# The passage from sampling to attention in a four-image hybrid block: image 0's last two tiles projected alone, the other images' projections behind the second scores

## The reference, cut to what matters

```python
x = x + _L0_conv_ref(_gn(x), ...)        # ends: out @ out_w + out_b
t = _to_tokens(x)                        # (4, 1024, 128)
t = t + _L1_attn_ref(_ln_t(t), W)        # x = n @ W; softmax(x @ n.T / sqrt(128)) @ n
t = t + _L1_ffn_ref(_ln_t(t), ...)       # router, two experts, gelu, layer norm
```

## Time and profile before

| | us |
|---|---|
| median of 3 runs | 721.9 (720.75 to 722.38) |
| profiled execution, its own time | 724.42 |
| its span, first to last instruction | 722.7 |
| mean granted clock of PE in it | 0.908 of full |

### The profile page before, as it was taken

One profiled execution on the slowest core, in us unless ns is written; L12 is line 12 of the kernel. 1 busy time (PEld: TensorE's weight loads), 2 busy tenths in 40 slices (PEclk: granted clock), 3 DMA queues, 4 the chain that ended last, 5 costly groups with the idle time before them and its releaser, 6 DMA issues.

```text
span 722.7 us, 11093 instructions
## 1 busy us (share of the span) xinstructions
PE 593.9 (82%) x3456; PEld 444.2 (61%) x3456; DVE 580.6 (80%) x1052; ACT 227.1 (31%) x332; POOL 306.8 (42%) x326
## 2 busy tenths in 40 slices
PE   4982878869859869869959589779999999939995
PEld 3452656557547558557547477647777777725674
DVE  4489899998997997998999999456777766752766
ACT  6150502413314314215206000144445444413431
POOL 7523795897348793058068240021221221125111
PEclk9796988998998987988999779989999999977998
DMA  6057503003003006000000000000000000004111
GB/s 182 29 212 269 169 1 103 3 1 103 1 1 103 2 2 254 1 1 2 1 1 3 0 1 1 1 0 1 1 1 1 1 0 1 1 3 115 30 45 44
DMA packets 25595, 30.54 MB, mean 42 GB/s; under 512 B 5189, under 2 KB 17685, under 8 KB 25557
## 3 DMA queue, kind: packets, MB, share of 16 engines
q1 hardware_dynamic: 24654, 29.77, 12.5%
q0 software_dynamic: 896, 0.23, 0.4%
q10 hardware_dynamic: 6, 0.00, 0.0%
HBM read 24.94 MB, written 5.05 MB: 42 GB/s over the span
## 4 chain that ended last, share of the span: by engine, by line
PE 55%; DVE 20%; issue 10%; DVEq 2%; ACT 1%; POOL 0%; POOLq 0%; ACTq 0%
PE banks L777 14%; DVE prod L1355 9%; PE banks L887 8%; PE pair L867 8%; PE pair L932 4%; PE pair L730 4%; PE banks L877 4%; PE banks L966 3%; DVE stencil L1331 3%; DVE outer L1325 3%; PE banks L795 3%; PE pair L723 2%; PE banks L793 2%; PE banks L859 1%; DVE hats L1292 1%
## 5 line engine op out<-in xcount | busy, mean ns | idle before, releaser
L777 PE MATMUL banks<-ident,prod 128*128 128x128 f32 x1568 | 225.2, 295 | 81.5 <-DVE prod L1355 80.8
L777 PEld LDWEIGHTS banks<-ident,prod 128*128 128x128 f32 x1568 | 192.7, 152 | 136.1 <-DVE prod L1355 112.5
L1355 DVE TENSOR_TENSOR prod<-shifted,stencil 128x1024 f32 (+1 forms) x224 | 238.8, 1089 | 17.3 <-PE banks L777 14.5
L1123 POOL CAST far_list_i<-far_list 1x8 int32<-1x8 f32 x8 | 40.5, 5066 | 105.5 <-DVE far_list L1341 86.1
L1151 POOL TENSOR_TENSOR rstd_now<-mv_now,neg_half 128x2 f32<-128x2 f32 x32 | 22.9, 717 | 135.6 <-DVE mv_now L1407 135.6
L730 PE MATMUL pair<-xg,dw_diag 128*128 128x512 f32 x144 | 73.4, 611 | 1.7 <-ACT dw_diag L511 1.7
L887 PEld LDWEIGHTS banks<-shifted 128*128 128x128 f32 x512 | 60.2, 192 | 8.1 <-issue 6.1
L887 PE MATMUL banks<-shifted 128*128 128x128 f32 x512 | 63.3, 277 | 2.3 <-ACT shifted L639 1.4
L1325 DVE TENSOR_TENSOR outer<-hats 128x800 f32<-128x800 f32 x64 | 63.2, 987 | 0.8
L1331 DVE TENSOR_TENSOR stencil<-stencil,outer 128x800 f32 (+1 forms) x64 | 62.9, 983 | 0.3
L867 PE MATMUL pair<-shifted 128*128 128x512 f32 x128 | 60.4, 596 | 0.6 <-ACT shifted L622 0.6
(11 more groups left out here) (229 smaller groups left out, 871.6 us busy)
## 6 DMA issues: line engine op xcount, KB each, us to landing
shifted<-padded SPq DMA_DIRECT2D x42, 256.0 KB
shifted<-padded SPq DMA_DIRECT2D x14, 640.0 KB
res<-in_x_dram SPq DMA_DIRECT2D x4, 512.0 KB, 5.7
padded<-stage SPq DMA_DIRECT2D x4, 512.0 KB, 2.7
stage<-in_L_ffn_W_dram SPq DMA_DIRECT2D x16, 128.0 KB, 2.1
out_dram<-res SPq DMA_DIRECT2D x8, 256.0 KB, 2.3
padded<-stencil SPq DMA_DIRECT2D x2, 228.0 KB, 2.5
got<-padded,cell_now POOLq DMA_INDIRECT x28
```

What stands on the lines that cost most here:

```text
L777: mm = pe.matmul(acc_of(c, r), prod[:, d % PROD, r * G:(r + 1) * G, :].rearrange("p g c -> p (g c)"), ident[:, :], is_transpose=True, star ...
L1123: gp.tensor_copy(far_list_i[:, :], far_list[:, :]).then_inc(point, 1)
L1355: ins = ve.tensor_tensor(prod[:, dx:dx + n, :, :], shifted[:, dx:dx + n, bass.ds(((c % HALF) * ROWS + dy) * G, ROWS * G), :], stencil_of[: ...
```

## The change

The projection of the last two chunks (6 and 7) is split by image. Behind `add_fix` of chunk 7, PE projects image 0 of chunk 6 and then image 0 of chunk 7, three matmul calls each; chunk 7 has its own copy of samples (`samp_last`, behind `samp_t` in `xg`) and its own bank (bank 1), so ACT makes both sample copies one behind the other. Two residual copies of one tile follow (`res1_first`). DVE waits for the residuals of chunks 0 to 5 ahead of the first statistics, for `res1_first` ahead of those of pair 3, and for all residuals ahead of the attention loop. On PE the transposes and keys of image 0 come first, then the scores of tile 0, the keys of pair 3, the scores of tile 1, the projections of images 1 to 3 of both chunks, and then pairs 4 and 5. ACT has the residuals of images 1 to 3 between the two exponentials. The banks of pairs 2 and 3 move from `pair[0]` to `pair[1]`.

```diff
-            first = [bank[2], bank[3], pair[0][:, 0:512], pair[0][:, 512:1024], bank[2], bank[3]]
+            first = [bank[2], bank[3], pair[1][:, 0:512], pair[1][:, 512:1024], bank[2], bank[3]]
...
-            for k in (CHUNKS - 2, CHUNKS - 1):
-                copy_out(k)
-                residual(k)
+            def residual_of(k, n0, n1):
+                at = k % 2
+                sc.activation(res[:, :, :].rearrange("p (n k) c -> p n k c", n=B)[:, n0:n1, k, :],
+                              bank[at][:, n0 * P:n1 * P].rearrange("p (n c) -> p n c", c=C), ACT.Copy
+                              ).then_inc(res1_first if n0 == 0 else res1_done, 1)
+
+            copy_out(CHUNKS - 2)
+            copy_out(CHUNKS - 1)
+            for i, k in enumerate((CHUNKS - 2, CHUNKS - 1)):
+                sc.wait_ge(conv_first, i + 1)
+                residual_of(k, 0, 1)
...
             copy_normed(0)
-            for j in range(LEAD):
-                if j + 1 < LEAD:
-                    copy_normed(j + 1)
+            copy_normed(1)
+            copy_keys(0)
+            copy_normed(2)
+            copy_keys(1)
+            copy_normed(3)
+            copy_keys(2)
+            copy_keys(3)
+            exps(0, 0)
+            for i, k in enumerate((CHUNKS - 2, CHUNKS - 1)):
+                sc.wait_ge(conv_out, CHUNKS - 1 + i)
+                residual_of(k, 1, B)
+            exps(1, 1)
+            for j in (4, 5):
+                copy_normed(j)
                 copy_keys(j)
-                if j == 3:
-                    exps(0, 0)
-                    exps(1, 1)
...
-            def project(k):
+            def project(k, n0=0, n1=B):
+                last = isinstance(k, int) and k == CHUNKS - 1
                 pe.wait_ge(samp_t_done, k + 1)
-                pe.wait_ge(res1_done, k + 1)
-                for n in range(B):
-                    y = bank[0][:, n * P:(n + 1) * P]
+                pe.wait_ge(res1_done, CHUNKS - 1 if last else k + 1)
+                if n0 > 0:
+                    pe.wait_ge(res1_first, 2 if last else 1)
+                for n in range(n0, n1):
+                    y = bank[1 if last else 0][:, n * P:(n + 1) * P]
...
-            add_up(CHUNKS - 1, AT_SAMPLES, AT_PROJECT)
-            project(CHUNKS - 2)
-            add_up(CHUNKS - 1, AT_PROJECT, STENCIL)
+            add_up(CHUNKS - 1, AT_SAMPLES, STENCIL)
             add_fix(CHUNKS - 1)
-            project(CHUNKS - 1)
+            project(CHUNKS - 2, 0, 1)
+            project(CHUNKS - 1, 0, 1)
...
             normed_to_t(0)
-            for j in range(LEAD):
-                if j + 1 < LEAD:
-                    normed_to_t(j + 1)
+            pe.wait_ge(samp_t_done, CHUNKS)
+            normed_to_t(1)
+            keys(0)
+            normed_to_t(2)
+            keys(1)
+            normed_to_t(3)
+            keys(2)
+            pe.wait_ge(normed_t1, TILES // 2)
+            pe.wait_ge(keyed_done, 1)
+            scores(0, 0)
+            keys(3)
+            pe.wait_ge(keyed_done, TILES // 2)
+            scores(1, 1)
+            project(CHUNKS - 2, 1, B)
+            project(CHUNKS - 1, 1, B)
+            for j in (4, 5):
+                normed_to_t(j)
                 keys(j)
-                if j == 3:
-                    pe.wait_ge(keyed_done, 4)
-                    scores(0, 0)
-                    scores(1, 1)
+            pe.wait_ge(res1_done, CHUNKS + 1)
...
-            ve.wait_ge(res1_done, CHUNKS + 1)
+            ve.wait_ge(res1_done, CHUNKS - 1)
...
+                    if j + 1 == TILES // 2 - 1:
+                        ve.wait_ge(res1_first, 2)
                     token_stats(j + 1, 2 * ((j + 1) % 2), var1)
...
             maxima(1, 1)
+            ve.wait_ge(res1_done, CHUNKS + 1)
```

More of the change, by code:

```diff
@@ L240, in hybrid_block_kernel @@
         fix = over_stage[:, :].rearrange("p (s g c) -> p s g c", s=CHUNKS, c=CG)
-        samp_t = xg[:, :, :, :].rearrange("p y w n -> p (y w n)")[:, 0:CT].rearrange("c (n r w) -> c n r w", n=B, r=ROWS)
+        samp_t, samp_last = [xg[:, :, :, :].rearrange("p y w n -> p (y w n)")[:, s * CT:(s + 1) * CT]
+                             .rearrange("c (n r w) -> c n r w", n=B, r=ROWS) for s in range(2)]
         over_shifted = shifted[:, :, :, :].rearrange("p d s c -> p (d s c)")
@@ L350, in hybrid_block_kernel @@
         res1_done = sem("res1_done")
+        res1_first = sem("res1_first")
+        conv_first = sem("conv_first")
         var1 = sem("var1")
@@ L560, in copy_out @@
                 sc.wait_ge(samp_tp, k + 2)
-                sc.activation(samp_t, banks[:, bass.ds(512 + (k % 2) * 1024, 512)].rearrange("c (r w n) -> c n r w", r=ROWS, n=B),
+                sc.activation(samp_last if isinstance(k, int) and k == CHUNKS - 1 else samp_t, banks[:, bass.ds(512 + (k % 2) * 1024, 512)].rearrange("c (r w n) -> c n r w", r=ROWS, n=B),
                               ACT.Copy).then_inc(samp_t_done, 1)
@@ L786, in add_fix @@
                 mm.then_inc(samp_tp, 1)
-            def project(k):
+            def project(k, n0=0, n1=B):
+                last = isinstance(k, int) and k == CHUNKS - 1
                 pe.wait_ge(samp_t_done, k + 1)
-                pe.wait_ge(res1_done, k + 1)
-                for n in range(B):
-                    y = bank[0][:, n * P:(n + 1) * P]
-                    pe.matmul(y, samp_t[:, n, :, :].rearrange("c r w -> c (r w)"), out_w_sb[:, :], start=True, stop=False)
+                pe.wait_ge(res1_done, CHUNKS - 1 if last else k + 1)
[3 more added lines that the diff above has]
+                    y = bank[1 if last else 0][:, n * P:(n + 1) * P]
+                    pe.matmul(y, (samp_last if last else samp_t)[:, n, :, :].rearrange("c r w -> c (r w)"), out_w_sb[:, :],
+                              start=True, stop=False)
                     pe.matmul(y, ones16[0:3, :], bias_parts3[:, 3 * GP:], start=False, stop=False)
                     mm = pe.matmul(y, ident[:, :], res[:, n * TILES + k, :], start=False, stop=True)
-                mm.then_inc(conv_out, 1)
+                mm.then_inc(conv_out if n1 == B else conv_first, 1)
             pe.wait_ge(gate_done, 1)
```

## The result

| | before | after |
|---|---|---|
| median of 7 runs, us | 721.9 (719.71 to 724.77) | 717.2 (716.22 to 721.9) |
| ratio, 95% interval | | 0.995 (0.9927 to 0.9973) |
| profiled execution, us | 724.42 | 716.8 |
| its span, us | 722.7 | 714.9 |
| mean granted clock of PE | 0.908 | 0.921 |

The forecast was 717.7. A ratio of 0.995 is 3.6 us, between 1.9 and 5.3. The two profiled executions differ by 7.6 us (their spans by 7.8), and that is not the change's doing alone: the last product ended at 458.99 us before and at 454.42 after, in code that no edit touches. Of the 7.8 us the passage up to the loop's first scores gave 3.00, the sampling stage ahead of it 4.57, the rest 0.23.

A forecast was written before the change was run, and what follows sets the result against it. Latency of the chain from sampling's last product to the attention loop was taken as the bound: 10.85 us gained at the first scores less 6.65 given back is 4.2, so 721.9 - 4.2 = 717.7 us, range 716.0 to 720.9.

The forecast's parts named there:

- Reading the chain: From the last sampling product to the attention loop's first turn: latency bounds; bringing the loop forward brings the end forward equally.
- Step 1, DVE's start: DVE's first statistics, waiting only for chunks 0 to 5, begin at 459.05 instead of 467.98: 8.93 us earlier.
- Step 2, PE and ACT ahead of the norm: Behind the last products: sample copy from 460.36, one-tile residuals by 462.32, transpose of pair 0 at 461.81, costing nothing.
- Step 3, the first scores: First scores behind the norm of pair 3 start at 467.26 against 478.11: 10.85 us earlier, full clock kept.
- Step 4, what is given back: Between first scores and loop, 6.65 us given back, most of it 4.80 of projections; keys of pair 5 at 480.41.
- The hole of 0.6 ahead of the second scores: PE waits about 0.6 us, as the copy of pair 3's keys now follows the first scores.
- ACT's in-order price: Tile 1's exponential, free to run at 473.3, stands behind both residuals on ACT until 477.44 and ends at 478.54.
- The sum: Keys of pair 5 at 480.4 instead of 484.64: 4.2 us less, bounds 3.8 to 4.5.
- the first rival: Half clock before the scores or at 477.1 to 480.4: costs 1.75 us, gain 2.45, time 719.4; chance 0.25.
- the second thin place: Stretch 477.1 to 480.4 ahead of the loop, where PE has only two pairs' short work; half clock possible there.
- the first sparse stretch: Norm passage before the scores, PE working 0.82 us of each 1.50 for four pairs; full clock assumed.
- the prediction's own list: Signs to check: first scores 10.9 us earlier, probability transposes about 4.2 earlier; wrong if half clock from the first scores on.

The follow-up runs named there:

- the two experiments on single orders: Changed kernel with pair 3's keys ahead of the first scores, 716.77 us; changed kernel with tile 1's exponential ahead of both residuals on ACT, 718.40 us.
- both experiments that kept the two gaps: Changed kernel with DVE's first statistics waiting for both one-tile residuals, 726.01 us; changed kernel with pair 3's keys ahead of the first scores, 716.77 us.
- keys of pair 3 first: Changed kernel with the keys of pair 3 ahead of the first scores on PE, all else as changed; 716.77 us in its one run.
- the split alone: Changed kernel with DVE waiting for both one-tile residuals ahead of its first statistics, all else as changed; 726.01 us in its one time.
- exponential first: Changed kernel with the exponential of tile 1 ahead of the two residuals on ACT instead of behind them; 718.40 us in its one run.
- The second set of runs: Kernel before, changed kernel and kernel before with only DVE's waits changed, 12 runs each on one chip: medians 722.06, 719.11 and 718.46 us.
- early start: Kernel before with only DVE's waits changed: chunks 0 to 5 ahead of first statistics, all residuals ahead of pair 3's; 716.27 us, ratio 0.9941.

## Why the prediction was right, step by step

*Reading the chain.* That the passage is a chain of latencies, and that what it loses comes off the end, held: from the loop's scores to the end 236.42 after, 236.65 before, a difference smaller than the 1.8 us by which this stretch varies over the twelve profiles.

*Step 1, DVE's start.* Forecast 8.93 us earlier; 9.07 by distance (8.99 against -0.08). The row of the statistics begins 0.08 before that of the last product ends.

*Step 2, PE and ACT ahead of the norm.* Forecast: transpose of pair 0 at 2.82 behind the last product; measured 3.01. The one-tile residuals took 0.28 each, the value taken. Slack for pair 3's statistics was 0.5, forecast 0.8; it was enough.

*Step 3, the first scores.* 10.85 forecast, 11.01 measured. The clock, on which this step and a rival rested, stayed full in the stretch 458 to 462. The Trainium skill (TensorE: Matmul & The Clock Gate, "A second HAM failure mode: psum-queue depth-cycling") has frequent short idle gaps between groups of matmuls make the clock swing; in this stretch, with gaps of 0.83, 0.56 and 0.62 us, it did not.

*Step 4, what is given back.* By distance, forecast and measured: second scores 11.15 and 11.08; end of the projections 17.67 and 17.70; second residual 17.96 and 17.90; exponential 18.45 and 18.28; keys of pair 4 19.99 and 19.81; keys of pair 5 21.42 and 21.34. The hole of 0.6 ahead of the second scores is there (0.56), and so is ACT's in-order price; the two experiments on single orders put 0.77 and 1.09 on them. The largest error of this step is 0.18.

*The sum.* 4.2 us at the keys of pair 5, 4.31 measured. Up to the loop's scores only 3.00, since the half clock took 1.32. That was the first rival, given 0.25, and at the second thin place it came in both profiles of the changed kernel and in both experiments that kept the two gaps; 0.25 was too low. Its price was put at 1.75. Counted to the scores of the loop's next turn, it was 1.4 in both profiles of the changed kernel, 1.7 with the keys of pair 3 first, and 3.1 in the split alone, where the low stretch lasted 6.8 us instead of 3.4: not one figure, but one that differs between executions. Here the same section of the Trainium skill (TensorE: Matmul & The Clock Gate) agrees with the trace in part: 1.2 GHz followed on a short gap, one of 1.73 us. But gaps of 0.64 and 0.62 us at the same place (exponential first) and one of 2.17 us (before) were not followed by it. I had weighed that rule at the first sparse stretch alone, where it did not hold.

*The time.* 717.7 forecast, 717.2 measured, well inside the range, but with luck: the passage gave 3.0, the median 4.7. The 1.7 between them lies inside the interval of the ratio (1.9 to 5.3 us); the sampling stage, whose end moves by 5 us between profiles (below), is the likely source, though no timed run shows it. By the prediction's own list it would be wrong if windows show half clock anywhere from the first scores on, and they do (0.70 and 0.63): the order of the work and the waits were forecast rightly, the clock was not. The first probability transposes came 3.83 us earlier by distance, where the list has about 4.2. The second set of runs, 719.11 against 722.06, gives 2.95, nearly the passage's own 3.00.

*What the prediction did not see.* It read the two edits, early norm and split, as one. Its own step 1 and rows held the better statement: the statistics of pair 3 only had to move from 472.04 to 467.98 for a gain of 4.06, with nothing split. With the early start in place, the split and the moved projections add 0.25 at the keys of pair 5 and, by the half clock that comes with them, leave it 1.07 behind at the loop's scores.

## What to carry to other kernels

Before moving work to shorten a chain, ask what each stage really needs of the stage before, and lower that wait first: two lines gave 4.06 of the 4.31 us, and at the loop's scores more than the whole change (4.07 against 3.00). Then place displaced work in the hand-overs that already wait, a piece in each, instead of in one block behind the critical step; a block of 4.8 us with bare hand-overs behind it cost its own length, the hand-overs and the clock. On an in-order engine look at each instruction that is ready and stands behind one that waits.

## What the runs showed of the hardware that was not expected

The same sampling code ended at 454.4 to 455.4 us in eight profiles and at 459.0 to 459.4 in four, of kernels before and after alike. Windows of the stretch 213.6 to 224 us, first the kernel before in its first profile, then in its second:

```profile
213.60:224.00 10.40, 10.03 (x42) 8.67 (x43) 7.79 (x9) 2.11 (x2) 6.74 (x9) 0.51 0.31 94
```

```profile
213.60:224.00 10.40, 10.40 (x69) 8.69 (x68) 10.21 (x12) 2.12 (x2) 7.88 (x9) 0.87 0.42 132
```

With half clock PE shows 42 instead of 69 matmul records there, and DVE is busy 7.79 instead of 10.21 us. The four late profiles read 0.51 to 0.53, the eight early ones 0.84 to 0.90; in the 7.6 us just ahead (206 to 213.6), where PE has less to do, it is the other way round, 1.00 in the four and 0.72 to 0.94 in the eight. That this stretch makes the larger part of the difference is read from ACT's timelines. In the two profiles of the kernel before, the sample copy of chunk 1 begins at 205.99 and 205.72, the copy into `far_counts` behind the stretch at 240.07 and 236.10: 0.3 us apart ahead of it, 4.0 behind, of 4.1 at the last product. Between the first profiles of before and changed the same two copies are 1.6 (205.99 and 204.41) and 4.4 us apart (240.07 and 235.68), of 4.6. Why one execution is granted the clock there and another is not stays open; nothing that I ran steers it.

Half clock came in four profiles of four in which PE had the gaps of 1.73 and 0.61 us with 0.9 us of work between them. It fell at the start of the second gap in three of them and behind it, 0.25 us into the keys of pair 5, in the fourth (keys of pair 3 first), so that the second gap is not shown to be needed. It was low for 3.4 us in three and for 6.8 in the fourth. One gap of 2.17 or 2.18 us between dense stretches brought it in none of four (before and early start, two profiles each), nor did two gaps of 0.64 and 0.62 us (exponential first).
